# Attention with mixture of experts on one core: row maxima turned by VectorE in 32 by 32 blocks, and three score tiles of a pass in a fourth bank

## The reference

```python
xn = layernorm(x)
q, k, v = (heads(xn @ W.T + b) for W, b in ((Wq, bq), (Wk, bk), (Wv, bv)))   # [8, 16, 1024, 64]
att = softmax(q @ k.T / sqrt(64))
x + (att @ v) @ Wo.T + bo + moe(xn)
```

## Time and profile before

| | us |
|---|---|
| median of three runs | 3530.04 |
| the profiled execution | 3532.16 |
| its span, first to last instruction | 3530.4 |
| PE busy | 3450.2 (98%) |
| POOL busy | 2731.7 (77%) |
| DVE busy | 2426.9 (69%) |
| ACT busy | 1643.5 (47%) |
| PE, all L831 and L834 (2048 each) | 878.6 and 812.6 |
| DVE, all reduces L1132 (1024) | 1205.5 |

### The profile page before, as it was taken

One profiled execution on the slowest core, in us unless ns is written; L12 is line 12 of the kernel. 1 busy time (PEld: TensorE's weight loads), 2 busy tenths in 40 slices (PEclk: granted clock), 3 DMA queues, 4 the chain that ended last, 5 costly groups with the idle time before them and its releaser, 6 DMA issues. The chain is left out here.

```text
span 3530.4 us, 60337 instructions
## 1 busy us (share of the span) xinstructions
PE 3450.2 (98%) x16416; PEld 2076.7 (59%) x16416; DVE 2426.9 (69%) x3127; ACT 1643.5 (47%) x3058; POOL 2731.7 (77%) x2339
## 2 busy tenths in 40 slices
PE   7999799999999999999999999999999999999699
PEld 6888555555555555555555555555555555555487
DVE  7888577667667776776767676666667677666344
ACT  4555344444444444444444444444444444444343
POOL 2111289999999999999999999999999998999421
PEclk9999799999999999999999999999999999999899
DMA  7777856766666666666777677766766666663486
GB/s 246 240 220 218 218 126 161 184 186 184 184 183 184 185 184 184 184 182 182 187 188 188 185 188 188 185 185 180 186 184 186 186 186 184 184 183 95 158 317 226
DMA packets 418253, 669.15 MB, mean 190 GB/s; under 512 B 56288, under 2 KB 222880, under 8 KB 418208
## 3 DMA queue, kind: packets, MB, share of 16 engines
q1 hardware_dynamic: 395424, 637.13, 64.8%
q0 software_dynamic: 14336, 23.08, 3.4%
q10 hardware_dynamic: 8448, 8.39, 0.7%
HBM read 306.91 MB, written 126.12 MB: 123 GB/s over the span
## 5 line engine op out<-in xcount | busy, mean ns | idle before, releaser
L1132 DVE TENSOR_REDUCE merged<-psum 128x1 f32<-128x1024 f32 x1024 | 1205.5, 1219 | 670.3 <-PE psum L860 592.8
L1095 ACT ACTIVATE probs<-psum 128x512 f32<-128x512 f32 x2048 | 1085.0, 600 | 1215.3 <-PE psum L834 1209.3
L1321 POOL TENSOR_TENSOR sums<-sums,probs 128x512 f32<-128x512 f32 x768 | 1001.1, 1303 | 62.4 <-ACT probs L1095 3.3
L1322 POOL TENSOR_TENSOR sums<-sums,probs 128x512 f32<-128x512 f32 x768 | 981.9, 1279 | 0.0
L875 PE MATMUL psum<-probs,v_sb 128*64 128x512 f32 x4096 | 936.1, 599 | 0.0
L831 PE MATMUL psum<-q_full,k_full 128*128 128x512 f32 x2048 | 878.6, 429 | 0.9 <-DVE low L1142 0.9
L834 PE MATMUL psum<-q_rest,k_rest 65*128 65x512 f32 x2048 | 812.6, 397 | 1.4 <-DMA q_rest<-minus_max 1.4
L875 PEld LDWEIGHTS psum<-probs,v_sb 128*64 128x64 f32 x4096 | 271.6, 136 | 563.0 <-issue 501.3
L831 PEld LDWEIGHTS psum<-q_full,k_full 128*128 128x128 f32 x2048 | 388.4, 190 | 197.4 <-issue 75.0
L834 PEld LDWEIGHTS psum<-q_rest,k_rest 65*128 65x128 f32 x2048 | 390.0, 190 | 62.5 <-DMA q_rest<-minus_max 1.7
L936 PE MATMUL psum<-x_t,w_qk 128*128 128x512 f32 x1536 | 409.7, 403 | 12.9 <-DVE merged L1132 6.7
(11 more groups left out here) (154 smaller groups left out, 3079.9 us busy)
## 6 DMA issues: line engine op xcount, KB each, us to landing
x_t<-xt SPq DMA_DIRECT2D x118, 1024.0 KB, 6.8
k_full<-high SPq DMA_DIRECT2D x256, 256.0 KB
v<-values SPq DMA_DIRECT2D x64, 512.0 KB, 3.5
w_qk<-wqk_parts SPq DMA_DIRECT2D x64, 512.0 KB
v_sb<-v SPq DMA_DIRECT2D x64, 512.0 KB, 4.8
q_full<-high SPq DMA_DIRECT2D x128, 256.0 KB
q_full<-low SPq DMA_DIRECT2D x128, 256.0 KB
k_rest<-low SPq DMA_DIRECT2D x128, 256.0 KB
```

The lines of the kernel that those rows point to most:

```text
L1095: nc.scalar.activation(probs[:, kt, h, :], ring[ring_place(g, j) % RING], ACT.Exp, scale=SCALE).then_inc(probs_ready, 1)
L1132: nc.vector.tensor_reduce(out=merged[:, col:col + 1], in_=work[:, 2 * h:2 * h + 2, :].rearrange("p b c -> p (b c)"), axis=AX, op=ALU.max, ...
L1321: nc.gpsimd.tensor_tensor(total[:, 0, :], first[:, 0, :], probs[:, kt, 0, :], ALU.add)
L1322: nc.gpsimd.tensor_tensor(total[:, 1, :], first[:, 1, :], probs[:, kt, 1, :], ALU.add).then_inc(sums_added, 1)
```

## The change

- Table `ITEMS`: the item MT is gone from slots 0 and 2, with its transpose on PE, the semaphores `turn_filled`, and the same transpose in the head of the stage.
- `shift` on DVE waits for its own reduces (`quad_reduced`) and turns [128, 32] of `merged` in four blocks of 32 by 32 within SBUF (`turned`). It stands right behind the reduces of the slot, ahead of the fillers; it stood behind them.
- `shift_out` on SP issues four DMAs, one per block (8 rows of 32 numbers each), where it issued one. Every wait for `shift_placed` counts four.
- The fifth score tile of slots 1, 2 and 3 (tiles 12, 20, 28) goes into bank 7. It waits for the reduces of the odd quad before it, and the even quad after it waits for its exponential. The ring of three banks serves the other 29 tiles and the sums.

```diff
-ITEMS = ({2: "PJ", 3: "MT", 5: "XT"}, {2: "PJ", 4: "GU"}, {2: "PJ", 3: "MT"}, {2: "PJ", 5: "DN"})
+ITEMS = ({2: "PJ", 5: "XT"}, {2: "PJ", 4: "GU"}, {2: "PJ"}, {2: "PJ", 5: "DN"})
...
+BLOCK = 32
+TURNS = P // BLOCK
+
+WORK_TILES = tuple(8 * g + 4 for g in range(1, SLOTS))
+RING_TILES = [m for m in range(SCORES) if m not in WORK_TILES]
+USERS = RING_TILES[:SUM_PLACE] + ["sum"] + RING_TILES[SUM_PLACE:]
...
+    def score_bank(j):
+
+        return work[:, 3, :] if j in WORK_TILES else ring[USERS.index(j) % RING]
...
-    merged = sb("merged", [P, P + 2 * GROUP])
-    minus_max = sb("minus_max", [2 * GROUP, 2, P], F32R)
+    merged = sb("merged", [P, 2, BLOCK], F32R)
+    turned = sb("turned", [P, 2, BLOCK], F32R)
...
-            ring_free(s, place, fin)
+            out = score_bank(j)
+            if j in WORK_TILES:
+                pe.wait_ge(quad_reduced, at_most(QUADS * (s + 1) + 4 * g, QUADS * NP))
+            else:
+                ring_free(s, USERS.index(j), fin)
...
+                if att and 8 * g + 4 in WORK_TILES:
+                    pe.wait_ge(probs_ready, SCORES * s + 8 * g + 5)
                 if att and g == 0:
                     pe.wait_ge(xt_copied, s + 1)
-                    pe.wait_ge(shift_ready[1], s + 1)
...
-                if g == 2:
-                    pe.wait_ge(shift_ready[0], s + 2)
...
-            elif name == "MT":
-                half = 0 if g == 2 else 1
-                pe.wait_ge(quad_reduced, reduced)
-                nc.tensor.transpose(work[:, 2, 0:P], merged[:, 2 * GROUP * half:2 * GROUP * half + P], ident[:]).then_inc(turn_filled[half], 1)
...
-        def shift(p, half, bank=None):
-            if bank is None:
-                bank = work[:, 2, :]
-            dve.wait_ge(turn_filled[half], p + 1)
+        def shift(p, half):
+            dve.wait_ge(quad_reduced, QUADS * p + 2 * GROUP * (half + 1))
             if not known(p, 1):
-                dve.wait_ge(shift_placed[half], DMA * p)
-            nc.vector.tensor_copy(minus_max[:, half, :], bank[0:2 * GROUP, 0:P]).then_inc(shift_ready[half], 1)
+                dve.wait_ge(shift_placed[half], DMA * TURNS * p)
+            nc.vector.transpose(f32(turned[:, half, :]), f32(merged[:, half, :])).then_inc(shift_ready[half], 1)
...
-                for name in FILLERS[g][0]:
-                    filler(s, par, flags, name)
                 if g == 0 and att:
                     shift(s, 1)
                 if g == 2 and nxt:
                     shift(s + 1, 0)
+                for name in FILLERS[g][0]:
+                    filler(s, par, flags, name)
...
-            sp.dma_start(f32(q_rest[DK:DK + 1, par, half, :, :]), f32(minus_max[:, half, :])
-                         ).then_inc(shift_placed[half], DMA)
+            for b in range(TURNS):
+                to = q_rest[DK:DK + 1, par, half, :, :].rearrange("o h (q b i) -> o (h q) b i", b=TURNS, i=BLOCK)[:, :, b, :]
+                sp.dma_start(f32(to), f32(turned[BLOCK * b:BLOCK * b + 2 * GROUP, half, :])
+                             ).then_inc(shift_placed[half], DMA)
```

More of the change, by code:

```diff
@@ L648, in at_most @@
     return min(v, most) if isinstance(v, int) else v
-def ring_place(g, j):
-    return j + (g >= 1)
 SUM_PLACE = 8
 SPREAD = 8
-def ring_before(s, place, fin):
[L662 to L666, removed]
+BLOCK = 32
[3 more added lines that the diff above has]
+USERS = RING_TILES[:SUM_PLACE] + ["sum"] + RING_TILES[SUM_PLACE:]
+assert len(USERS) % RING == 0
+def ring_before(s, place, fin):
+    user = USERS[place - RING]
+    if user == "sum":
         if fin:
             return "sum", s
-        before -= RING
-    return "score", SCORES * s + before - (before > SUM_PLACE) + 1
+        user = USERS[place - 2 * RING]
+    return "score", SCORES * (s if place >= RING else s - 1) + user + 1
 def one(ap, i, pattern, out):
@@ L821, in score @@
             half, kt, j = g // 2, GROUP * (g % 2) + i, 8 * g + 2 * i + h
-            place = ring_place(g, j)
-            out = ring[place % RING]
-            ring_free(s, place, fin)
+            out = score_bank(j)
[3 more added lines that the diff above has]
+                ring_free(s, USERS.index(j), fin)
             if j == 0:
@@ L832, in score @@
             if g % 2 == 0 and i == 0 and h == 0:
-                pe.wait_ge(shift_placed[half], DMA * (s + 1))
+                pe.wait_ge(shift_placed[half], DMA * TURNS * (s + 1))
             nc.tensor.matmul(out, k_rest[:, par, h, keys], q_rest[:, par, half, h, :],
@@ L970, in second_project @@
             def second_project(g):
-                if g == 1:
-                    pe.wait_ge(shift_ready[0], 1)
                 if g == 2:
@@ L1001, in head @@
             pe.wait_ge(rows_out, 8)
-            pe.wait_ge(quad_reduced, 2 * GROUP)
-            nc.tensor.transpose(psum[:, 3, 0:P], merged[:, 0:P], ident[:]).then_inc(turn_filled[0], 1)
             first_quad(4)
@@ L1094, in exp @@
                     act.wait_ge(sums_added, added)
-            nc.scalar.activation(probs[:, kt, h, :], ring[ring_place(g, j) % RING], ACT.Exp, scale=SCALE
+            nc.scalar.activation(probs[:, kt, h, :], score_bank(j), ACT.Exp, scale=SCALE
                                  ).then_inc(probs_ready, 1)
@@ L1110, in step @@
                         exp(s, g, n // 2, n % 2)
-                    if ITEMS[g].get(n, "MT") != "MT" and present(ITEMS[g][n], g, flags):
+                    if n in ITEMS[g] and present(ITEMS[g][n], g, flags):
                         item(s, par, g, ITEMS[g][n])
@@ L1121, in _ @@
         nc.vector.memset(ones[:], 1.0).then_inc(set_up, 1)
-        nc.vector.memset(merged[:], 0.0).then_inc(set_up, 1)
+        nc.vector.memset(f32(merged[:]), 0.0).then_inc(set_up, 1)
         nc.vector.memset(hidden[:], 0.0).then_inc(set_up, 1)
@@ L1130, in reduce @@
                 dve.wait_ge(quad_filled, QUADS * (s + 1) + 2 * q + h + 1)
-                col = 2 * GROUP * (q // GROUP) + GROUP * h + q % GROUP
-                nc.vector.tensor_reduce(out=merged[:, col:col + 1],
+                col = GROUP * h + q % GROUP
+                nc.vector.tensor_reduce(out=merged[:, q // GROUP, col:col + 1],
                                         in_=work[:, 2 * h:2 * h + 2, :].rearrange("p b c -> p (b c)"),
@@ L1263, in head @@
             table()
-            shift(0, 0, psum[:, 3, :])
+            shift(0, 0)
             reduce(-1, 4)
@@ L1355, in shift_out @@
             else:
-                alone(sp, (standing, 1), (shift_placed[half], DMA * p), (shift_ready[half], p + 1))
-            sp.dma_start(f32(q_rest[DK:DK + 1, par, half, :, :]), f32(minus_max[:, half, :])
-                         ).then_inc(shift_placed[half], DMA)
+                alone(sp, (standing, 1), (shift_placed[half], DMA * TURNS * p), (shift_ready[half], p + 1))
+            for b in range(TURNS):
+                to = q_rest[DK:DK + 1, par, half, :, :].rearrange("o h (q b i) -> o (h q) b i", b=TURNS, i=BLOCK)[:, :, b, :]
+                sp.dma_start(f32(to), f32(turned[BLOCK * b:BLOCK * b + 2 * GROUP, half, :])
+                             ).then_inc(shift_placed[half], DMA)
         def spread_out(p):
```

4 lines of the change are left out of this document (removed).

## The result

The changed kernel takes **3518.83 us**, median of 7 runs (3516.92 to 3520.89), beside 3530.04 for the kernel before (7 runs, 3528.47 to 3532.01). The ratio is 0.9968, with a 95% interval of 0.9959 to 0.9977: 11.2 us less. The forecast was 3517.6 us, 12.4 less. The profiled execution took 3520.27 us.

A forecast was written before the change was run, and what follows sets the result against it. PE was taken to set the pace. 0.10 + 0.09 + 0.03 - 0.02 = 0.20 us a step, over 62 regular steps 12.4 us, gave 3530.04 - 12.4 = 3517.6 us; range 3508 to 3526.

The forecast's parts named there:

- MT off PE, slot 2: Slot 2 on PE: removing the transpose saves 0.10 us a step; tile 20's inherited wait for the reduces costs nothing.
- One more bank: Slot 2: tiles 22 and 23 stop waiting for exponentials, saving 0.09 us; slots 1 and 3 gain nothing.
- MT off PE, slot 0: Slot 0: removing the 0.10 us transpose gains only 0.03 us, since the quad waits for ACT's copy of XT.
- The turn on DVE: Slot 2: block transpose takes d = 0.20 us, hidden in 0.24 of room before the quad; 0.02 us a step charged.
- SP: SP's queue: three more issues, twice a step, take 1.9 to 2.6 us in slot 0; cost zero.
- The rest: Head and last steps: tiles 12 and 28 may wait, MT's wait goes; zero, give or take 1 us.
- DVE takes over in slot 2: Rival: low_part arrives after PE and eats the gain; at d = 0.40, 0.06 us a step, 3526; chance 0.13.
- All of it shows: Rival: ACT's copy in slot 0 does not hold the quad, d small; 0.29 us a step, 18 us, 3512; chance 0.17.
- The wait was never there: Rival: tiles 22 and 23 are stretched by something other than the ring; 0.11 us a step, 3523; chance 0.09.
- SP's queue: Rival: small DMA issues cost like large ones, making NORM0 late; at 1.6 us each, +22 us, 3552; slower side 0.09.
- No idle weights with ACT as the releaser: Sign for slot 2 of the changed kernel: no weights held idle with ACT named as releaser.
- within 0.06 us of the end of L1134 or later than it by more: Sign for slot 2: when the even quad would start relative to the end of L1134.

The follow-up runs named there:

- experiment 2: Changed kernel with all score tiles back in the ring of three banks, turn still on VectorE: 3523.97 us, ratio 0.9981.
- experiment 3: Kernel before, transpose still on TensorE, with only tiles 12, 20 and 28 moved to bank 7: 3521.53 us, ratio 0.9974.
- experiment 4: Kernel before, with the quads' wait for the reduces and its register operation moved ahead of the late waits: 3525.55 us, ratio 0.9988.
- Experiment 7: Changed kernel with slot 2's turn behind low_part, plus ACT's copy of XT ahead of tile 5's exponential in slot 0: 3506.77 us, ratio 0.9935.
- experiment 5: Changed kernel with each of the four shift_out DMAs split by head, eight issues per half, same bytes: 3562.1 us, ratio 1.0093.
- experiment 6: Changed kernel with a second block transpose into an unread spare tile ahead of the real one: 3519.81 us, ratio 0.9971.
- experiment 1: Changed kernel with the turn of slot 2 moved behind low_part, nothing else: 3511.07 us, ratio 0.9941.

## Why the prediction was right, and where not

The total was right (12.4 us forecast, 11.2 measured; 0.20 us a step forecast, 0.208 measured). That it came out so near was luck: two of the terms were off by 0.13 and 0.08 us a step, in opposite directions. Per step:

| | forecast | measured |
|---|---|---|
| slot 2: transpose off PE | -0.10 | -0.13 |
| slot 2: the ring | -0.09 | -0.09 |
| slot 2: the quad held | +0.02 | **+0.15** |
| slot 0: transpose off PE, less the quad held | -0.03 | -0.11 + 0.05 = -0.06 |
| slot 1 | 0 | 0.00 |
| slot 3 | 0 | **-0.08** |
| sum | -0.20 | -0.21 |

The measured terms are differences of mean times between matmul starts, rounded to 0.01; the step itself is 0.208 shorter. (Slot 1's distance fell by 0.01 us, but its other matmuls took that back.)

1. *MT off PE, slot 2.* Right, the term a little larger. Tile 20's inherited wait for the reduces costs nothing in any looped step.
2. *One more bank.* Right in size. But it counts only if the quad behind it isn't held: in experiment 2, without it, slot 2 takes only 0.02 us longer. It did count in experiment 3. And "in slots 1 and 3 nothing is to be had" was wrong for slot 3: not by a stretch of its tiles, but by the order of the waits at its quad (experiment 4). Rows of slot 3 of the kernel before show 0.40 us where 0.32 were needed. I had looked at score tiles only, not at that distance.
3. *MT off PE, slot 0.* The mechanism was right: the quad waits for ACT's copy and follows it by 0.10 us, in both kernels. The size was put at 0.03 because the quad seemed already to be waiting before. It wasn't by more than 0.01 (0.335 against 0.32), so half of the gain came through. Experiment 7 collects the rest.
4. *The turn on DVE.* **This is the step that failed.** Its price was right: forecast d = 0.20, measured 0.21 us, with the next instruction 0.21 after its start. All 128 turns in one row:

```profile
L1142 DVE STREAM_TRANSPOSE turned<-merged x128: 203/211/215, 400.2 to 3243.1; 128x32 f32<-128x32 f32 x128
```

   It started 0.12 us after the end of the reduces (0.14 forecast), and `low_part` ended 0.21 us later behind the reduces than before (d = 0.20 forecast). Wrong was "less a hop of some 0.05 between engines", a number that I chose and took from no row. From the end of `low_part` to the quad 0.24 or 0.25 us pass, in four kernels (the changed one, experiments 2, 5 and 6). The order of instructions on PE has a register operation and further waits behind the wait for `lows_ready`. The trace's records of PE's queue show them in the changed kernel, counted from the end of `low_part`: the register operation at 0.04 us, the next wait from 0.13 to 0.18, the quad's weights at 0.21, the quad at 0.24. Where the late wait has nothing behind it, at ACT's copy in slot 0, 0.10 us pass. Whether `low_part` too would be followed by 0.10 us if its wait stood last, no run tried. By the forecast's own times, 2024.19 + 0.24 = 2024.43 against 2024.28: 0.15 late, the 0.15 that was measured. The forecast's warning, "if d were 0.29, 0.05 would be lost", had the right mechanism with the wrong threshold: the room was 0.05 us, not 0.24.

   The Trainium skill ("VectorE: DVE Perf Modes", The three transpose paths) gives 311 ns for VectorE, on 128 x 128 bf16. The 211 ns here are for 128 x 32 float32, a quarter of the columns, so the two do not contradict each other, and its figure used as d would have been too high.
5. *SP.* Right that it costs nothing. The three more issues took 3.77 - 0.88 = 2.9 us in slot 0 (1.9 to 2.6 forecast) and left the queue without idle time. Less the 1.3 us of idle time that they used up, they made `sum_all` at most 1.6 us late, within the room of 2.7 that landing and NORM0 allow. Experiment 5 shows how near the edge is.
6. *The rest.* Tiles 12, 20 and 28 wait for DVE only in the last steps, by 1.6 us in all.

*The rivals.* "DVE takes over in slot 2" happened, in part: `low_part` sets the quad's time in every looped step, at 0.15 us. It was hidden from the total by slots 3 and 0. "All of it shows" needed two more moves, experiments 1 and 7, and then gives still more than its 18 us, since slot 3 comes on top. "The wait was never there" is out: the stretch went in experiment 3. "SP's queue" needs more than four issues.

The signs named ahead of the run fared as follows. The distances of the score tiles, the copy's 0.10 us, the turn's price, the punctual `sum_all` and the two steps closer by 0.4 us came true. "No idle weights with ACT as the releaser" held for the score tiles; at the quad's weights the trace names ACT with 0.47 us of idle time, and there the name is wrong. The last, the quad "within 0.06 us of the end of L1134 or later than it by more", could not tell the cases apart, since the quad followed by 0.24 us while it was held.

Turning on VectorE is worth about 10 us once it stands behind `low_part` (experiment 1 against 3). As the change was made, it was worth 2.7 (the changed kernel against 3), and the rest of its gain came from the bank: from its own tiles and from the order of the waits that it brought along.

## What to carry to other kernels

For each instruction of the bounding engine that waits for another, measure the distance from its predecessor against the smallest such distance in the same program, in all repetitions of the pattern, before looking for costs: it finds what is held (here slot 3) without trusting the named releaser. Work inserted on an engine that isn't the bound belongs behind the instruction for which the bounding engine waits. And when a "hop" between two engines enters a sum, take it from a row where the waiter is really held: with further waits and a register operation behind the one met last it was 0.24 us, five times the guess, and more than the whole room.

## What was not expected of the hardware

- A wait placed late in a list of waits, with its register operation behind the one that is met last, costs 0.07 to 0.08 us at the waiter (slot 3: 0.403 against 0.329, experiment 4). The share of the register operation alone was not measured.
- Two block transposes in a row on DVE cost 0.03 us more than one before the next instruction starts (experiment 6). The time between the first's start and NORM0's is nearly the same, so most of it isn't the transposes' own work. What fills it no run here shows.
- DVE's busy time rose by 26.5 us, though its instruction count is the same. The expert's `count_rows` scaling (128 x 128) went from a mean of 631 ns to 834, and the NORM operations (128 x 512) from 1046 to 1104. The longer ones stand beside GpSimd's additions, as SILU0 does in the five long steps of experiment 5 (1.35 to 1.38 us against 0.29). That the additions are the cause is argued from this, not tested; in the step shown above the same instruction takes 0.69 us as NORM0 (2013.88) and 1.53 as NORM1 (2019.58). The step did not grow by it. The groups of `count_rows` by line, in the kernel before and then in the changed one:

```profile
L1196 DVE TENSOR_SCALAR count_rows<-count_rows,rank 128x128 f32<-128x128 f32 x64 | 40.4, 631 | 8.4 <-DMA count_rows<-counts_rows,count_slot 8.4
```

```profile
L1186 DVE TENSOR_SCALAR count_rows<-count_rows,rank 128x128 f32<-128x128 f32 x64 | 53.4, 834 | 9.0 <-DMA count_rows<-counts_rows,count_slot 9.0
```

- Issues of small DMAs also differ with what goes ahead: 0.94 us each for four directly behind the large copies, 0.69 for the same four later in the step, 0.73 for eight in the first place, which carry half the rows each. Large copies and number of rows both differ there, and no run parts them.
- A pause of PE can cost more than its length. Behind a wait of 2.51 us the granted clock read 0.50 for 3.1 us (experiment 5). Behind four of the five waits of 2.2 us and more, work of 4.91 us took 6.4 to 6.6.
